# A masked copy moved from POOL to ACT in a fused sequence, attention and expert kernel

## The chip, the core and the metric

The kernel runs on one core of a Trainium2 chip. A core has a matrix engine (PE, whose weight loads are shown as PEld), a vector engine (DVE), an engine for activation functions (ACT), a general-purpose engine (POOL), and a queue engine (SP) that here only starts transfers. Each engine works through its own list of instructions in order; they wait for each other through counters (semaphores). PE writes its products into PSUM, eight banks of 512 float32 columns on 128 partitions. ACT and DVE read PSUM, POOL here reads and writes only SBUF. The metric is the device time of one execution in microseconds.

## The reference

The input is 128 sequences of 375 steps and 64 channels. Three blocks follow each other:

```
h = x
for i in 3 layers:                      # state-space layers
    dt, B, C = split(h @ W_dbc[i].T)    # 1 + 64 + 64 columns
    delta = softplus(dt * W_dt[i] + b_dt[i])
    hs = scan(exp(delta * A[i]) , delta * h * B)     # along time, 64 states
    h = sum_n(hs * C) + D[i] * h
    if i < 2: h = mean of neighbouring steps (375 -> 187 -> 93)
h = h + attention(layernorm(h))         # 8 heads, a polynomial of the scores, row-normalised
h = h + experts(layernorm(h))           # 6 experts of three layers, the 2 best are mixed
```

The router of the experts takes a softmax over six logits, the two largest probabilities, and a softmax over these two; with the difference of the two, its weights are 1/(1 + e) and e/(1 + e).

## The kernel before, in words

The 128 sequences are worked in 16 groups of eight. In a group there are four units of the state-space part: A and B are the first layer, four sequences each (744 columns of two banks); C is the second layer for all eight (744 columns), D the third (372 columns). Then follow "att" and "ffn" for the group. Layer 1 of group 5 may thus run while group 2 is in the experts. Only the first of the 64 states is scanned; the others are small enough that their part within one time step is a product with `m_quad`. A test at the end decides whether a general version has to run as well, which it doesn't for these inputs.

The order of the work is written out by hand, one list for each engine, in `ORDER` (line 222). An entry such as `B.three:4` is the step "three" of unit B in group 4; an entry of PE also names the PSUM bank that its product takes (`B.row:4/4`). Each step asks for what it needs with `need(g, ...)`; a wait is issued only if the counter has not been seen that far. Nothing overtakes within an engine.

The steps that matter here, for one unit:

- PE "row" (line 1235): the few projections of x that every channel needs (dt, and B and C of the first state) become rows, each of them three times, on partitions of one PSUM bank.
- ACT "row" (line 972) copies this bank to SBUF as float32, `rows`: 128 partitions, 186 columns (93 for D). DVE "most" takes a maximum of it for the test.
- POOL "three" (lines 879 to 885) splits the copies into three bfloat16 parts, so that a bfloat16 product can carry them: the masked high part, the difference, the masked middle part, and the last difference, which is `rows_three`. `row_mask` holds two columns of zeros and ones per partition, made by DVE in "prep.back".
- PE "dpre", "b" and "c" (line 1246) multiply `rows_three` by a matrix of zeros and ones and so spread each row over 64 channels.
- ACT "exp", "ln" and "decay" make delta and the decay; POOL "du" (line 889) is delta times x; DVE "vin", "scan" (line 1703), "base", "based" and "carry" (line 1716) make the output; POOL "y" (line 896) adds the two parts, and POOL "pooled" (line 904) adds neighbouring steps for the next layer.

SP loads x and swaps its halves (line 775). In attention, DVE makes normalised queries and keys (line 1762), POOL spreads the queries over the heads (`q_exp`, line 911), PE makes the scores (line 1348), ACT squares them (`pm`, line 1051), PE multiplies by the values (line 1361). In the experts, ACT makes the hidden layers (lines 1086 and 1093), DVE weights them (line 1818), PE makes the output (line 1456). DVE's "gate" (lines 1809 to 1813) turns the router's result into weights: `st` is a small SBUF tile, while `key` and `rsum` lie in the PSUM bank of the router's logits. POOL "split" (line 922) splits these weights as "three" splits the rows.

The wait that stands ahead of POOL's "three", and ACT's "row":

```
need(g_, f"act {u}.row")
need(0, "dve prep.back")
need(g_, f"pe {u}.dpre", f"pe {u}.b", f"pe {u}.c", back=1)
...
need(g, f"pe {u}.row")
need(g, f"pool {u}.three", f"dve {u}.most", back=1)
a.activation(rows[u][:], out_of(f"{u}.row", g)[:, 0, 0:WIDE[u] // 2], ACT.Copy).then_inc(me, 1)
```

Of the kernel before, what the change touches and what calls it, by code (L numbers as in the profile page):

```python
# [27 lines left out]
P = 128  # L28
# [8 lines left out]
def audio_tower(nc, x, A_log, Dp, W_dbc, W_dt, b_dt, Wqkv, bqkv, Wproj, bproj, temperature,  # L37
# [24 lines left out]
    with ctx:  # L62
# [88 lines left out]
        def per_unit(name, extra=0):  # L151
# [514 lines left out]
        def out_of(job, g):  # L666

            return ring[:, BANK[job, g]:BANK[job, g] + JOBS[job][0]]
# [813 lines left out]
        def _(dve):  # L1482
# [295 lines left out]
            def experts(g, u, s):  # L1778
                norm(g, u, s)

                def step(ins, name):

                    ins.then_inc(me, 1)
                    need(g, f"dve ffn.{name}")
# [76 lines left out]
```

## Time and profile before

| what | value |
|---|---|
| median of 3 timed runs | 685.24 us (682.52 to 686.23) |
| the profiled execution | 687.21 us |
| its span, first to last instruction | 685.4 us |
| mean granted clock of PE | 0.954 of full speed |
| PE / DVE / ACT / POOL busy | 583.1 / 560.9 / 517.7 / 470.6 us |
| HBM read, written | 13.25 MB, 3.05 MB |

The page and the trace come from one profiled execution. "Busy" is time in which an engine runs an instruction; waits on semaphores and starts of DMAs don't count. A matmul's end is modelled. The chain that ended last is followed back from the last instruction, at each step to what released it or to the instruction before it on its engine; "issue" on it is time for which the profile shows no wait. A wait for several counters is put down to the one that came last.

### The profile page before, as it was taken

Reading aid. Unit: us, or ns where it says so; the run is one execution under the profiler, and the core shown is the slowest. Engines: PE = TensorE matmul, PEld = TensorE weight load, DVE = VectorE, ACT = ScalarE, POOL = GpSimd, SP = SyncE. Lnnn points to the kernel's source line nnn. Section 1 sums busy time; section 2 is a strip of 40 time slices with the busy share of each in tenths; the row PEclk is TensorE's granted clock in tenths of the full one; section 3 lists DMA queues with packets and bytes.
Section 4 is the critical chain, followed back from the end, with each engine's and each line's share of the span. In section 5 each row is a group of like instructions: output and inputs, shape, how many; then the busy total and the mean of one; then the engine's idle time right before and its main releaser. Section 6 shows DMA issues by size and latency. Waiting matters only on the chain.

```text
span 685.4 us, 22980 instructions
## 1 busy us (share of the span) xinstructions
PE 583.1 (85%) x9595; PEld 306.5 (45%) x9595; DVE 560.9 (82%) x1097; ACT 517.7 (76%) x964; POOL 470.6 (69%) x564
## 2 busy tenths in 40 slices
PE   2857666889989898999999898998999988999983
PEld 1322233545445444554545444554545444545431
DVE  6799788889979798998998898999789888764551
ACT  1335548879969888998897887978888887897751
POOL 7769999889767778786886787786686775322000
PEclk9975879999999999999999999999999999999996
DMA  4422321221112202121211203121121000000001
GB/s 89 83 58 64 69 61 41 46 53 25 41 35 68 54 13 66 39 56 46 55 37 26 62 17 82 36 64 33 33 57 30 2 14 18 20 13 14 2 14 27
DMA packets 77576, 28.54 MB, mean 42 GB/s; under 512 B 69271, under 2 KB 77463, under 8 KB 77463
## 3 DMA queue, kind: packets, MB, share of 16 engines
q1 hardware_dynamic: 71290, 25.92, 16.5%
q10 hardware_dynamic: 6173, 1.05, 0.8%
q8 instruction: 78, 1.28, 0.8%
q14 instruction: 35, 0.29, 0.1%
HBM read 13.25 MB, written 3.05 MB: 24 GB/s over the span
## 4 chain that ended last, share of the span: by engine, by line
PE 45%; POOL 22%; ACT 12%; DVE 11%; issue 6%; DMA 2%; ACTq 1%; SPq 0%; POOLq 0%; DVEq 0%
PE ring L1260 6%; PE ring L1348 4%; PE ring L1361 4%; PE ring L1427 4%; PE ring L1436 4%; PE ring L1456 3%; ACT pm L1051 3%; PE ring L1246 3%; PE ring L1215 2%; PE ring L1235 2%; PE ring L1329 1%; ACT hid L1093 1%; PE ring L1270 1%; DVE ring L1707 1%; POOL q_exp L911 1%
## 5 line engine op out<-in xcount | busy, mean ns | idle before, releaser
L1051 ACT ACTIVATE pm<-ring,two_col 93x744 f32<-93x744 f32 x128 | 106.9, 872 | 13.1 <-PE ring L1348 12.0
L911 POOL TENSOR_TENSOR q_exp<-qk,mask_q 128x1488 f32<-128x1488 f32 x16 | 42.9, 2684 | 28.9 <-DVE qk L1762 28.9
L1348 PE MATMUL ring<-q_exp,qk 32*93 32x372 f32 x512 | 56.2, 507 | 7.4 <-POOL q_exp L911 0.9
L1086 ACT ACTIVATE hid<-ring,b_col 128x372 f32<-128x372 f32 x96 | 49.4, 567 | 7.7 <-PE ring L1436 6.3
L1818 DVE TENSOR_TENSOR hidw<-hid,ring 128x744 f32<-128x744 f32 x48 | 44.3, 922 | 12.2 <-PE ring L1417 8.9
L1361 PE MATMUL ring<-pm,v 97*32 97x93 f32 x2048 | 53.9, 247 | 0.1
L1361 PEld LDWEIGHTS ring<-pm,v 97*32 97x32 f32 x2048 | 42.9, 111 | 16.0 <-ACT pm L1051 4.8
L1093 ACT ACTIVATE hid<-ring,b_col 128x744 f32<-128x744 f32 x48 | 42.2, 878 | 7.4 <-PE ring L1427 5.4
L1427 PE MATMUL ring<-hid,w 64*64 64x372 f32 x384 | 40.9, 496 | 2.9 <-ACT hid L1086 2.0
L1436 PE MATMUL ring<-nrm_f,w 64*64 64x372 f32 x384 | 41.7, 505 | 0.7 <-ACT hid L1093 0.5
L896 POOL TENSOR_TENSOR base_C<-base_C,carry_C 128x744 f32<-128x744 f32 x16 | 28.5, 1780 | 18.0 <-DVE carry_C L1716 14.8
L896 POOL TENSOR_TENSOR base_A<-base_A,carry_A 128x744 f32<-128x744 f32 x16 | 28.3, 1770 | 11.4 <-DVE carry_A L1716 11.3
L1456 PE MATMUL ring<-hidw,w 128*64 128x372 f32 x192 | 34.3, 494 | 0.0
L889 POOL TENSOR_TENSOR du_A<-delta_A,x_A 128x744 f32<-128x744 f32 x16 | 28.7, 1797 | 7.7 <-ACT delta_A L989 7.7
L889 POOL TENSOR_TENSOR du_B<-delta_B,x_B 128x744 f32<-128x744 f32 x16 | 28.8, 1799 | 7.2 <-ACT delta_B L989 5.7
L889 POOL TENSOR_TENSOR du_C<-delta_C,x_C 128x744 f32<-128x744 f32 x16 | 28.8, 1797 | 6.9 <-ACT delta_C L989 6.9
L922 POOL CAST gate_part<-gate 93x144 bf16<-93x144 f32 x16 | 4.8, 302 | 38.8 <-DVE gate L1813 38.7
L896 POOL TENSOR_TENSOR base_B<-base_B,carry_B 128x744 f32<-128x744 f32 x16 | 28.4, 1775 | 3.0 <-DVE carry_B L1716 3.0
L1348 PEld LDWEIGHTS ring<-q_exp,qk 32*93 32x93 f32 x512 | 17.2, 154 | 26.1 <-issue 4.6
L1703 DVE TENSOR_TENSOR_SCAN carry_B<-dec_B,ring 128x744 f32<-128x744 f32 x16 | 27.2, 1700 | 0.3
L1703 DVE TENSOR_TENSOR_SCAN carry_A<-dec_A,ring 128x744 f32<-128x744 f32 x16 | 27.2, 1698 | 0.2
L1703 DVE TENSOR_TENSOR_SCAN carry_C<-dec_C,ring 128x744 f32<-128x744 f32 x16 | 27.1, 1693 | 0.1
(368 smaller groups left out, 1816.7 us busy)
## 6 DMA issues: line engine op xcount, KB each, us to landing
xin_A<-in_x_dram SPq DMA_DIRECT2D x62, 93.0 KB
xin_B<-in_x_dram SPq DMA_DIRECT2D x62, 93.0 KB
x_A<-x_A SPq DMA_DIRECT2D x32, 93.0 KB, 2.4
x_B<-x_B SPq DMA_DIRECT2D x32, 93.0 KB, 2.2
x_C<-x_C SPq DMA_DIRECT2D x32, 93.0 KB, 2.2
out_dram<-osb SPq DMA_DIRECT2D x15, 186.0 KB
x_D<-x_D SPq DMA_DIRECT2D x32, 46.5 KB, 1.9
w<-in_L_ffn_expert_w_dram SPq DMA_DIRECT2D x6, 48.0 KB
```

What stands on the lines that cost most here:

```text
L889: g.tensor_tensor(halves(du[u][:]), halves(delta[u][:]), xs[u][:, 0::2, :], ALU.mult).then_inc(me, 1)
L896: g.tensor_tensor(base[u][:], base[u][:], carry[u][:], ALU.add).then_inc(me, 1)
L911: g.tensor_tensor(q_exp[:], qk[:, 0, :].rearrange("p (q t) -> p q t", q=NPAIR)[:, :, None, :].broadcast_to(wide), mask_q[:, None, :, None] ...
L1051: a.activation(pm[q % 2][h][0:TOUT].rearrange("m a j n -> m a (j n)"), out_of(f"att.s{q}{h}", g)[0:TOUT, :, 0:COLS], ACT.Square, bias=two_ ...
L1086: ins = a.activation(hid1[:, h], out_of(f"ffn.h1_{k}", g)[:, h, 0:COLS], ACT.Relu, bias=b1_col[:, h, k:k + 1])
L1093: a.activation(hid2[:], out_of(f"ffn.h2_{k}", g)[:, :, 0:COLS], ACT.Relu, bias=b2_col[:, k:k + 1]).then_inc(me, 1)
L1348: ins = mm(o[h][0:TOUT, b, 0:COLS], qk[r:r + 32, 1, q * TOUT:(q + 1) * TOUT], q_exp[r:r + 32, q].rearrange("p j n -> p (j n)"), start=True ...
L1361: ins = mm(o[32 * j:32 * j + 32, 0, h * TOUT:h * TOUT + TOUT], rows[:, at:at + 32], pm[q % 2][h][:, b, j, :], start=(b == 0), stop=(b == 1 ...
L1427: ins = mm(o[to:to + E, h, 0:COLS], w2[r:r + E, k, h], hid1[r:r + E, h], start=True, stop=True, tile_position=(r, to))
L1436: ins = mm(o[E * i:E * i + E, h, 0:COLS], w1[E * h:E * h + E, 2 * k + i], hn[E * h:E * h + E, :], start=True, stop=True, tile_position=(E ...
L1456: ins = mm(o[E * h:E * h + E, 0, 0:COLS], w3[:, k], hidw[k][:, h], start=False, stop=True, skip_group_check=True, tile_position=(0, E * h))
L1703: v.tensor_tensor_scan(carry[u][:], dec[u][:], b_made(u, g), 0.0, ALU.mult, ALU.add).then_inc(me, 1)
```

## The change

ACT's "row" makes two copies of the PSUM bank: `rows` as before, and `rows_hi`, in bfloat16 and scaled by the first column of the mask. POOL's "three" loses its first product. Its second product becomes a tensor_tensor with the mask's column broadcast, where it was a tensor_scalar. The wait for the masks ("prep.back") moves from POOL to ACT. In the gate, the denominator goes to `rsum` in PSUM instead of a column of `st`. The lists of all five engines are written anew: the same entries in another order, and other banks in PE's list. No entry of PE, ACT, POOL or SP moves more than 9 places; on DVE a few of the test's and the preparation's steps move further (up to 38).

Of the lists, the first lines of three engines:

```
-            "dve": ("prep.back:0 prep.w0:0 prep.mean:0 prep.dec:0 prep.w1:0 prep.w2:0 A.quad:0 B.most:0 prep.qkvp:0 "
-                    "B.quad:0 A.most:0 B.base:0 B.vin:0 B.based:0 B.scan:0 A.base:0 A.vin:0 B.carry:0 A.based:0 A.scan:0 "
-                    "prep.late:0 A.carry:0 B.quad:1 B.vin:1 prep.cen:0 B.scan:1 B.base:1 A.quad:1 B.based:1 B.carry:1 "
...
+            "dve": ("prep.w0:0 prep.back:0 prep.w2:0 prep.mean:0 prep.w1:0 B.most:0 A.most:0 prep.qkvp:0 prep.dec:0 "
+                    "B.quad:0 A.quad:0 B.base:0 B.vin:0 B.based:0 A.base:0 A.based:0 A.vin:0 B.scan:0 prep.late:0 "
+                    "B.carry:0 A.scan:0 A.carry:0 B.vin:1 B.scan:1 B.quad:1 prep.cen:0 C.most:0 B.base:1 B.carry:1 "
...
-            "pool": ("prep.pads0:0 prep.masks0:0 prep.masks1:0 B.three:0 A.three:0 prep.pads1:0 B.du:0 A.du:0 prep.pads2:0 "
-                    "B.three:1 B.y:0 B.pooled:0 B.du:1 A.y:0 A.pooled:0 C.three:0 A.three:1 C.du:0 B.y:1 A.du:1 B.three:2 "
...
+            "pool": ("prep.masks0:0 prep.masks1:0 A.three:0 B.three:0 prep.pads2:0 prep.pads1:0 B.du:0 A.du:0 prep.pads0:0 "
+                    "B.three:1 B.du:1 B.y:0 A.y:0 B.pooled:0 A.pooled:0 C.three:0 A.three:1 C.du:0 B.y:1 A.du:1 B.three:2 "
...
-            "act": ("A.x:0 prep.l3:0 B.x:0 prep.exp:0 A.row:0 B.row:0 prep.l5:0 B.exp:0 B.ln:0 B.decay:0 A.exp:0 A.ln:0 "
-                    "prep.l2:0 B.x:1 B.row:1 A.decay:0 B.exp:1 B.ln:1 A.x:1 B.decay:1 A.row:1 C.row:0 C.exp:0 C.ln:0 "
...
+            "act": ("prep.l3:0 A.x:0 B.x:0 prep.exp:0 A.row:0 B.row:0 prep.l5:0 B.exp:0 A.exp:0 B.ln:0 A.ln:0 prep.l2:0 "
+                    "B.x:1 B.decay:0 B.row:1 A.decay:0 B.exp:1 B.ln:1 A.x:1 B.decay:1 C.row:0 A.row:1 C.exp:0 C.ln:0 "
...
```

The rest of the diff:

```
@@ -577,7 +576,7 @@
                  "dve ffn.top": ["sum", "rsum", "key0", "kmax0", "oh0", "rest", "m1", "eq1", "key1", "kmax1", "oh1", "diff"],
                  "dve ffn.gate": ["den", "r0", "w1", "w", "gate"],
                  "pool ffn.split": ["hi", "mid", "rest", "lo"]}
-        PARTS |= {f"pool {u}.three": ["hi", "left", "mid", "three"] for u in UNITS}
+        PARTS |= {f"pool {u}.three": ["left", "mid", "three"] for u in UNITS}
 
         SSM_STEPS = ["sp swap", "pe row", "act row", "dve most", "pool three", "pe dpre", "act exp", "act ln", "dve delta", "pool du", "act decay",
                      "pe z", "dve quad", "pe b", "dve vin", "dve scan", "pe s", "dve base", "dve based",
@@ -873,14 +872,11 @@
             def ssm(g_, u, s):
                 if s == "three":
                     need(g_, f"act {u}.row")
-                    need(0, "dve prep.back")
                     need(g_, f"pe {u}.dpre", f"pe {u}.b", f"pe {u}.c", back=1)
                     r, hi, left, three = (t_[u][:] for t_ in (rows, rows_hi, rows_left, rows_three))
-                    g.tensor_scalar(hi, r, row_mask[:, 0:1], None, ALU.mult).then_inc(me, 1)
-                    need(g_, f"pool {u}.hi")
                     g.tensor_tensor(left, r, hi, ALU.subtract).then_inc(me, 1)
                     need(g_, f"pool {u}.left")
-                    g.tensor_scalar(hi, left, row_mask[:, 1:2], None, ALU.mult).then_inc(me, 1)
+                    g.tensor_tensor(hi, left, row_mask[:, 1:2].broadcast_to([P, WIDE[u] // 2]), ALU.mult).then_inc(me, 1)
                     need(g_, f"pool {u}.mid")
                     g.tensor_tensor(three, left, hi, ALU.subtract).then_inc(me, 1)
                 if s == "du":
@@ -969,7 +965,10 @@
                 if s == "row":
                     need(g, f"pe {u}.row")
                     need(g, f"pool {u}.three", f"dve {u}.most", back=1)
-                    a.activation(rows[u][:], out_of(f"{u}.row", g)[:, 0, 0:WIDE[u] // 2], ACT.Copy).then_inc(me, 1)
+                    need(0, "dve prep.back")
+                    made = out_of(f"{u}.row", g)[:, 0, 0:WIDE[u] // 2]
+                    a.activation(rows[u][:], made, ACT.Copy)
+                    a.activation(rows_hi[u][:], made, ACT.Copy, scale=row_mask[:, 0:1]).then_inc(me, 1)
                 if s == "exp":
                     need(g, f"pe {u}.dpre")
                     need(0, f"dve prep.w{l}")
@@ -1806,8 +1805,8 @@
                 if s == "gate":
                     need(g, "act ffn.topexp")
                     need(g, "pool ffn.lo", back=1)
-                    step(ts(st[:, 0], st[:, 6], 1.0, None, ALU.add), "den")
-                    step(v.reciprocal(st[:, 1], st[:, 0]), "r0")
+                    step(ts(rsum, st[:, 6], 1.0, None, ALU.add), "den")
+                    step(v.reciprocal(st[:, 1], rsum), "r0")
                     step(tt(key, key, spread(st[:, 6]), ALU.mult), "w1")
                     step(tt(key, oh0[:], key, ALU.add), "w")
                     tt(gate[:], key, spread(st[:, 1]), ALU.mult).then_inc(me, 1)
```

## Rows read from the trace of the kernel before

**Rows 1.** The page's part 1: busy us, share of the span, instructions.

```profile
PE 583.1 (85%) x9595; PEld 306.5 (45%) x9595; DVE 560.9 (82%) x1097; ACT 517.7 (76%) x964; POOL 470.6 (69%) x564
```

**Rows 2.** The page's part 4: shares of the chain that ended last, by engine.

```profile
PE 45%; POOL 22%; ACT 12%; DVE 11%; issue 6%; DMA 2%; ACTq 1%; SPq 0%; POOLq 0%; DVEq 0%
```

**Rows 3.** Windows: length, busy us (instructions) of PE, PEld, DVE, ACT, POOL; granted clock, DMA.

```profile
40.00:120.00 80.00, 54.94 (x726) 26.15 (x727) 70.04 (x103) 44.20 (x71) 72.23 (x77) 0.77 0.25 58
120.00:340.00 220.00, 199.75 (x3579) 107.43 (x3579) 196.81 (x330) 188.62 (x354) 172.39 (x192) 0.99 0.20 45
340.00:560.00 220.00, 202.60 (x3512) 107.76 (x3515) 195.39 (x344) 186.37 (x352) 165.58 (x191) 0.99 0.17 39
560.00:640.00 80.00, 76.18 (x1341) 41.25 (x1333) 50.73 (x139) 68.59 (x139) 27.36 (x32) 1.00 0.07 16
```

**Rows 4.** The chain that ended last, in order of time: start us, us, what.

```profile
20.80 0.78 POOL rows_hi_B L879
...
48.77 0.34 ACT rows_C L972
...
49.19 0.77 POOL rows_hi_C L879
...
109.07 2.64 POOL q_exp L911
...
556.94 0.54 POOL rows_hi_D L879
```

**Rows 5.** Waits of PE's matmuls, 120 to 560 us: us in total, times, longest.

```profile
PE ring L1246 <- POOL rows_three_D L885: 5.5, 7, 2.2
PE ring L1246 <- POOL rows_three_C L885: 3.9, 6, 1.4
PE ring L1246 <- POOL rows_three_B L885: 2.1, 3, 0.8
```

**Rows 6.** Timeline of POOL: start us, us, what; one three of C, one of D.

```profile
49.19 0.76 POOL L879 TENSOR_SCALAR rows_hi_C<-rows_C,row_mask 128x186 bf16<-128x186 f32 x1 [1.07 <-ACT rows_C L972]
50.03 0.54 POOL L881 TENSOR_TENSOR rows_left_C<-rows_C,rows_hi_C 128x186 f32<-128x186 f32 x1
50.67 0.76 POOL L883 TENSOR_SCALAR rows_hi_C<-rows_left_C,row_mask 128x186 bf16<-128x186 f32 x1
51.51 0.54 POOL L885 TENSOR_TENSOR rows_three_C<-rows_left_C,rows_hi_C 128x186 bf16<-128x186 f32 x1
...
67.25 0.54 POOL L879 TENSOR_SCALAR rows_hi_D<-rows_D,row_mask 128x93 bf16<-128x93 f32 x1
67.88 0.36 POOL L881 TENSOR_TENSOR rows_left_D<-rows_D,rows_hi_D 128x93 f32<-128x93 f32 x1
68.33 0.53 POOL L883 TENSOR_SCALAR rows_hi_D<-rows_left_D,row_mask 128x93 bf16<-128x93 f32 x1
68.94 0.36 POOL L885 TENSOR_TENSOR rows_three_D<-rows_left_D,rows_hi_D 128x93 bf16<-128x93 f32 x1
```

**Rows 7.** Groups of ACT's instructions: busy us, mean ns, idle before and its releaser.

```profile
L972 ACT ACTIVATE rows_C<-ring 128x186 f32<-128x186 f32 x16 | 5.2, 324 | 8.4 <-PE ring L1235 8.0
...
L972 ACT ACTIVATE rows_D<-ring 128x93 f32<-128x93 f32 x16 | 3.9, 245 | 3.6 <-PE ring L1235 3.6
...
L1012 ACT ACTIVATE ln_rows_a<-ring,eps_col 128x93 f32<-128x93 f32 x16 | 5.4, 338 | 0.7 <-PE ring L1277 0.7
...
L1034 ACT ACTIVATE qk_norm<-qk_norm,ln_col 128x186 f32<-128x186 f32 x16 | 7.1, 446 | 0.1
```

**Rows 8.** Timeline at 571 us: POOL's q_exp and DVE's denominator.

```profile
571.50 2.68 POOL L911 TENSOR_TENSOR q_exp<-qk,mask_q 128x1488 f32<-128x1488 f32 x1 [0.77 <-DVE qk L1762]
...
571.76 2.45 DVE L1809 TENSOR_SCALAR st<-st 93x8 f32<-93x8 f32 x1 [0.34 <-ACT st L1080]
```

**Rows 9.** The denominator's line 1809: ns min/median/max, first and last start us.

```profile
L1809 DVE TENSOR_SCALAR st<-st x16: 156/167/2446, 164.0 to 661.7; 93x8 f32<-93x8 f32 x16
```

**Rows 10.** Groups of DVE's instructions: the gate's product step; busy us, mean ns.

```profile
L1811 DVE TENSOR_TENSOR ring<-ring,st 93x48 f32<-93x48 f32 x16 | 3.4, 212 | 0.6
```

More of the change, by code:

```diff
@@ L579, in audio_tower @@
                  "pool ffn.split": ["hi", "mid", "rest", "lo"]}
-        PARTS |= {f"pool {u}.three": ["hi", "left", "mid", "three"] for u in UNITS}
+        PARTS |= {f"pool {u}.three": ["left", "mid", "three"] for u in UNITS}
         SSM_STEPS = ["sp swap", "pe row", "act row", "dve most", "pool three", "pe dpre", "act exp", "act ln", "dve delta", "pool du", "act decay",
@@ L875, in ssm @@
                     need(g_, f"act {u}.row")
-                    need(0, "dve prep.back")
                     need(g_, f"pe {u}.dpre", f"pe {u}.b", f"pe {u}.c", back=1)
                     r, hi, left, three = (t_[u][:] for t_ in (rows, rows_hi, rows_left, rows_three))
-                    g.tensor_scalar(hi, r, row_mask[:, 0:1], None, ALU.mult).then_inc(me, 1)
-                    need(g_, f"pool {u}.hi")
                     g.tensor_tensor(left, r, hi, ALU.subtract).then_inc(me, 1)
                     need(g_, f"pool {u}.left")
-                    g.tensor_scalar(hi, left, row_mask[:, 1:2], None, ALU.mult).then_inc(me, 1)
+                    g.tensor_tensor(hi, left, row_mask[:, 1:2].broadcast_to([P, WIDE[u] // 2]), ALU.mult).then_inc(me, 1)
                     need(g_, f"pool {u}.mid")
@@ L971, in ssm @@
                     need(g, f"pool {u}.three", f"dve {u}.most", back=1)
-                    a.activation(rows[u][:], out_of(f"{u}.row", g)[:, 0, 0:WIDE[u] // 2], ACT.Copy).then_inc(me, 1)
+                    need(0, "dve prep.back")
+                    made = out_of(f"{u}.row", g)[:, 0, 0:WIDE[u] // 2]
+                    a.activation(rows[u][:], made, ACT.Copy)
+                    a.activation(rows_hi[u][:], made, ACT.Copy, scale=row_mask[:, 0:1]).then_inc(me, 1)
                 if s == "exp":
@@ L1808, in experts @@
                     need(g, "pool ffn.lo", back=1)
-                    step(ts(st[:, 0], st[:, 6], 1.0, None, ALU.add), "den")
-                    step(v.reciprocal(st[:, 1], st[:, 0]), "r0")
+                    step(ts(rsum, st[:, 6], 1.0, None, ALU.add), "den")
+                    step(v.reciprocal(st[:, 1], rsum), "r0")
                     step(tt(key, key, spread(st[:, 6]), ALU.mult), "w1")
```

623 rows, old and new, of the table ORDER are left out of this document.

## The prediction, made before the changed kernel was run

> **What bounds the kernel now.** I read the busy line of the page first [rows 1]: PE 583 us, DVE 561, ACT 518, POOL 471 of a 685.4 us span. No engine is full on average, and POOL looks least pressed. The shares of the chain that ended last say otherwise [rows 2]: POOL holds 22% of it and ACT 12%, DMA only 2%. The reader is to see that the "spare" engine is on the path.
>
> The stretches show where [rows 3]. From 40 to 120 us POOL is busy 72.2 of 80, DVE 70.0, PE only 54.9 (at a granted clock of 0.77). This stretch is POOL's. From 120 to 560 us PE is busy 199.75 + 202.60 = 402.4 of 440 (91%), DVE 392.2 (89%), ACT 375.0 (85%), POOL 338.0 (77%): PE first, with DVE and ACT close behind. From 560 to 640 PE has 76.2 of 80 and POOL hardly works.
>
> The chain of waits in order of time [rows 4] shows which POOL work it is. The first step of a "three" (line 879, the masked high part) stands on the chain 43 times of 64, first at 20.80 and last at 556.94 us; the pieces add up to 29.4 us. The pieces of the third step (line 883) add up to 28.3 us. Before 24 of the 43 stands ACT's copy of the rows, as at 48.77. So a row product on PE goes to ACT, POOL and back to PE, and the end of the kernel often hangs on that loop. PE's own waits agree [rows 5]: from 120 to 560 us its matmuls of line 1246 waited 5.5 + 3.9 + 2.1 = 11.5 us for rows_three, in 16 waits, out of 37.6 us of idle time.
>
> **The change part by part.** The sum is made against the profiled execution, 687.21 us (span 685.4 and 1.8 around it). The median of the three timed runs is 685.24, so I work out a difference and take it off the median.
>
> *POOL loses the masked high part and does the masked middle part as a tensor_tensor.* Step times from start to start are in the timeline [rows 6]. For a unit of 186 columns: the high part 50.03 - 49.19 = 0.84 us, the difference 0.64, the middle 0.84, the last 0.54. The first goes, and the middle should take a tensor_tensor's 0.64: 0.84 + 0.20 = 1.04 us saved. For D (93 columns): 0.63 + (0.61 - 0.45) = 0.79. With 48 wide and 16 D steps, 48 x 1.04 + 16 x 0.79 = 62.5 us of POOL. The new middle step has an operand that is broadcast, which none of these rows has. Lower bound: q_exp, with both operands broadcast, took 2.68 us for 1488 columns [rows 8], 1.80 ns each, so 0.34 for 186, and the saving would be about 73 us. Upper bound: it stays at the tensor_scalar's 0.76, and the saving is 48 x 0.84 + 16 x 0.63 = 50.4. I take the tensor_tensor rows, the nearest in size and type.
>
> Against this edit speaks a rule of the Trainium skill. The page "GPSIMD Engine Reference" (sections "Performance versus the Vector engine" and "Engine selection") has two-input elementwise work bound by a shared read port at about 2.5 cycles an element, and one-input work roughly at line rate. By it (an estimate from that page) the middle step would become some 0.2 us dearer, POOL would save about 37 us, and the forecast below would be 680. The trace disagrees: for the same 186 columns the two-input step took 0.54 and the one-input step 0.76 [rows 6].
>
> *ACT gets a second copy from PSUM, with a scale read per partition.* The copy without it took 324 ns at 186 columns and 245 at 93 [rows 7]. Line 1012, 93 columns from PSUM with one per-partition operand, took 338: 93 ns more. So 0.417 and 0.338 us, and 48 x 0.417 + 16 x 0.338 = 25.4 us on ACT. Bounds: no extra cost, 48 x 0.324 + 16 x 0.245 = 19.5; line 1034's 446 ns for the wide ones, 26.8. 48 of the 64 fall between 120 and 560 us: 36 x 0.417 + 12 x 0.338 = 19.1, which takes ACT there to 394 of 440 (90%). Queued behind the second copy are the Exp, Ln and square steps that PE and POOL wait for, and the bank of the row product comes free one copy later. ACT's first row step now also waits for the masks ("back"), which DVE makes after "w0" instead of before it; PE's first row product ends at about 20 us, later than that work can end, so I cost it at nothing. Without that cover it would cost 1 to 3 us at the start.
>
> *The loop.* From PE's row product to PE's "dpre" the wide way gets 1.04 - 0.42 = 0.62 us shorter and D's 0.79 - 0.34 = 0.45.
>
> *What it is worth, stretch by stretch.* From 40 to 120 us eleven threes start (nine wide, two of D; the one at 49.19 [rows 4] is the first): 9 x 1.04 + 2 x 0.79 = 10.9 us off the busiest engine. DVE's 70.0 us is what is late next, so at most 10 can come through; I take 5.5, half. From 20 to 40 us the first two threes lie on the chain back to back, each 0.6 shorter: 1. From 120 to 560 us the 16 waits of PE can give at most 9 x 0.62 + 7 x 0.45 = 8.7 us (nine of the wide units, seven of D); late next is DVE or the PE work itself, so I take a third, 3, and charge 1 for the copies that ACT puts ahead of work that PE awaits: 2 net.
>
> *The gates' denominator.* One of its 16 instances took 2.45 us where the median is 0.17 [rows 8, 9]: it began 0.26 us after POOL's q_exp and ended with it, at 574.2. The gate's product step, which writes PSUM, took 0.21 us on average over its 16 [rows 10], so was never held up so; I expect the same of a denominator written there. That is 2.3 us at most, and PE has only 3.8 us of idle time between 560 and 640 us. I take 1; bounds 0 and 2.3.
>
> *New orders.* PE's order moves 489 of 872 entries (by 8 places at most), ACT's 526 of 789 (9), DVE's 484 of 686, POOL's 132 of 277, SP's 76 of 115 (6). SP's loads and swaps pass each other by a few places; with DMA at 2% of the chain, and x loaded ahead of use, I cost that at nothing, and at one late swap (2 to 3 us) if the cover goes. DVE's "late" preparation moves ahead of the first carry of B, which holds POOL's first sum; it may dodge the POOL work that it ran beside. I set both against each other. The orders as a whole can cost or return, by PE's idle 37.6 us, perhaps a fifth of it either way, 7.5 us; I take nothing.
>
> Sum: -5.5 - 1 - 2 - 1 = -9.5, so 677.7 for the profiled execution and 676 against the median.
>
> **The rivals.** *The chain shortens and nothing takes its place.* The chain loses 29.4 + 43 x 0.08 (the gaps) and a quarter of 28.3, and gains 24 copies of 0.4: -30 us, 655. For it: the 43 pieces. Against: in two thirds of the span PE and DVE are at 90%.
>
> *Nothing comes of it.* POOL only waits longer, for DVE's carries and ACT's deltas, the start gains 2 to 3 and the rest stays: 683. For it: the span is PE's and DVE's from 120 us on, and neither does less.
>
> *ACT becomes the bound (the other side).* Place: 120 to 560 us, ACT's queue. Price: 19 us of copies ahead of the squares, Exps and relus that PE waits for in order. If 10 of the 19 reach the end and the start gives 3: 692; all of them: 701. It turns slower than before once more arrives than the start gives, about 3 us, and measurably so from about 6.5, a third of the copies. For it: ACT at 90% beside PE at 91%, each in a fixed order. Against: ACT had 65 us idle there.
>
> **How the numbers follow.** A difference under 0.5% (3.4 us) can't be told from none. The forecast's own range, 668 to 681.8, has 0.55; the shortened chain (under 668) 0.10; nothing 0.20; ACT 0.15. Faster 0.65, same 0.20, slower 0.15. The range runs from 664, part of the way into the shortened chain, to 690, most of the way into ACT's case; the orders' 7.5 us and the bounds of the middle step lie within it.
>
> **What would show it.** POOL busy about 410 us, ACT about 543; the middle step at 0.54 and 0.36; the second copy at 0.42 and 0.34; no denominator above 0.3 us. The first q_exp, at 109.07 us before [rows 4], should start near 102. PE's waits for rows_three from 120 to 560 us should fall from 11.5 to 7 or less. I am wrong if the first q_exp comes no earlier than 106, if the stretch from there to the last three is not shorter, or if PE's waits for ACT's squares and Exps grow by more than its waits for rows_three shrink.

## The result, and the profile after

The changed kernel takes 658.25 us, median of four runs (656.1 to 659.24), against 684.76 before: ratio 0.961, with an interval of 0.9577 to 0.9643. The forecast was 676 with a range from 664 to 690, so the direction was right and the size was not: 26.5 us instead of 9.5. The profiled execution took 659.24 us with a span of 657.5.

First the parts of the page that answer to [rows 1, 2] (busy us by engine; shares of the chain that ended last):

```profile
PE 582.7 (89%) x9595; PEld 308.3 (47%) x9595; DVE 553.2 (84%) x1097; ACT 531.6 (81%) x1028; POOL 410.6 (62%) x500
...
PE 54%; ACT 16%; DVE 10%; POOL 7%; issue 5%; DMA 1%; SPq 0%; POOLq 0%; ACTq 0%; DVEq 0%
```

POOL's busy time fell by 60 us to 410.6, as worked out; its share of the chain fell from 22% to 7%. PE has the same work as before and now stands on 54% of the chain. ACT's busy time rose by 13.9 us, not 25, in the main because the second copy overlaps the first (below).

The stretches, as in [rows 3] (length, busy us of PE, PEld, DVE, ACT, POOL; clock, DMA):

```profile
40.00:120.00 80.00, 61.63 (x864) 30.29 (x862) 70.41 (x93) 51.20 (x90) 67.38 (x72) 0.78 0.24 56
120.00:340.00 220.00, 209.69 (x3696) 114.50 (x3696) 203.59 (x359) 202.72 (x398) 156.07 (x178) 1.00 0.21 50
340.00:560.00 220.00, 211.64 (x3703) 112.75 (x3706) 200.30 (x354) 200.96 (x393) 143.91 (x163) 1.00 0.17 39
560.00:640.00 80.00, 73.84 (x1171) 37.73 (x1167) 45.91 (x147) 62.33 (x129) 16.61 (x25) 1.00 0.05 11
```

From 120 to 560 us PE is busy 421.3 of 440 us, where it was 402.4. These windows hold different work in the two kernels, since everything comes earlier in the second. For a fair comparison take the stretch from the start of the first q_exp to the start of the thirteenth, nearly the same work in both (the lists move a few steps over its edges). Before:

```profile
109.02:543.52 434.50, 396.38 (x6960) 212.32 (x6960) 386.25 (x666) 369.91 (x694) 336.50 (x380) 0.99 0.19 44
```

After:

```profile
104.29:519.67 415.38, 396.29 (x6979) 213.72 (x6977) 384.29 (x669) 382.60 (x744) 293.05 (x333) 1.00 0.20 46
```

PE is busy 396.4 and 396.3 us in them, but 434.5 us pass before and 415.4 after: PE's idle time went from 38.1 to 19.1 us. So the gain in span of 27.9 us lies thus: 4.7 up to the first q_exp (109.02 to 104.29), 19.1 in this stretch, 4.1 behind it.

PE's waits for rows_three in it before (us in total, times, longest), as in [rows 5]:

```profile
PE ring L1246 <- POOL rows_three_D L885: 4.7, 6, 2.2
PE ring L1246 <- POOL rows_three_C L885: 3.9, 6, 1.4
PE ring L1246 <- POOL rows_three_B L885: 3.2, 4, 1.0
```

And the longest of PE's waits in it after:

```profile
PE ring L1347 <- POOL q_exp L907: 1.3, 2, 0.9
PE ring L1259 <- DMA x_D<-x_D: 1.1, 2, 0.7
PE ring L1347 <- ACT pm L1050: 0.8, 1, 0.8
```

rows_three is not among PE's waits any more; what is left are pieces of a microsecond or so from all sides.

The single prices. POOL's three of C in the timeline, as [rows 6]; then the second copy on ACT (ns min/median/max), beside [rows 7]; then the denominator, beside [rows 9]:

```profile
47.56 0.54 POOL L877 TENSOR_TENSOR rows_left_C<-rows_C,rows_hi_C 128x186 f32<-128x186 f32 x1 [1.35 <-ACT rows_hi_C L971]
48.17 0.49 POOL L879 TENSOR_TENSOR rows_hi_C<-rows_left_C,row_mask 128x186 bf16<-128x186 f32 x1
48.75 0.54 POOL L881 TENSOR_TENSOR rows_three_C<-rows_left_C,rows_hi_C 128x186 bf16<-128x186 f32 x1
```

```profile
L971 ACT ACTIVATE rows_hi_C<-ring,row_mask x16: 407/411/438, 47.1 to 542.8; 128x186 bf16<-128x186 f32 x16
L971 ACT ACTIVATE rows_hi_D<-ring,row_mask x16: 331/336/353, 65.8 to 565.1; 128x93 bf16<-128x93 f32 x16
```

```profile
L1808 DVE TENSOR_SCALAR ring<-st x16: 152/156/167, 155.8 to 633.3; 93x8 f32<-93x8 f32 x16
```

The middle product takes 0.49 us (0.54 forecast, 0.76 before), the copy with a scale 0.411 and 0.336 (0.417 and 0.338 forecast), and no denominator is longer than 0.167. The chain now goes round the loop like this (compare [rows 4]):

```profile
46.85 0.33 ACT rows_C L970
...
47.17 0.31 ACT rows_hi_C L971
...
47.56 0.55 POOL rows_left_C L877
...
48.17 0.49 POOL rows_hi_C L879
...
48.75 0.55 POOL rows_three_C L881
...
104.33 2.64 POOL q_exp L907
```

From the rows copy to the end of the last product it takes 2.44 us (46.85 to 49.29, in the chain's and the timeline's times), where from 48.77 to 52.05 it was 3.28.

### The profile page after: what moved, and what is told of

It reads as the page before. It is cut to its first block, busy times and chain, and to the rows that moved or that the text cites. A ratio compares the mean times of both kernels' runs of the same rounds, so it can differ in the third digit from the quotient of the medians.

```text
span 657.5 us, 22993 instructions
## 1 busy us (share of the span) xinstructions
PE 582.7 (89%) x9595; PEld 308.3 (47%) x9595; DVE 553.2 (84%) x1097; ACT 531.6 (81%) x1028; POOL 410.6 (62%) x500
## 4 chain that ended last, share of the span: by engine, by line
PE 54%; ACT 16%; DVE 10%; POOL 7%; issue 5%; DMA 1%; SPq 0%; POOLq 0%; ACTq 0%; DVEq 0%
PE ring L1259 8%; PE ring L1347 5%; PE ring L1360 5%; PE ring L1455 4%; PE ring L1245 3%; PE ring L1426 3%; PE ring L1435 3%; ACT pm L1050 3%; PE ring L1234 2%; PE ring L1406 2%; DVE ring L1706 2%; PE ring L1328 2%; PE ring L1214 2%; PE ring L1302 2%; ACT hid L1085 2%
## 5 line engine op out<-in xcount | busy, mean ns | idle before, releaser
L1435 PE MATMUL ring<-nrm_f,w 64*64 64x372 f32 x384 | 40.3, 488 | 0.7 <-DVE gate L1812 0.3
L964 ACT ACTIVATE x_A<-ring 128x744 f32<-128x744 f32 x16 | 12.6, 787 | 19.6 <-issue 14.7
L1057 ACT ACTIVATE yT<-ring 128x186 f32<-128x186 f32 x64 | 20.9, 326 | 8.7 <-PE ring L1360 8.1
```

Source lines behind the costliest of these rows:

```text
L1435: ins = mm(o[E * i:E * i + E, h, 0:COLS], w1[E * h:E * h + E, 2 * k + i], hn[E * h:E * h + E, :], start=True, stop=True, tile_position=(E ...
```

## The experiments

Each ran three or more times beside the kernel before on the same chip. The changed kernel's ratio, 0.961, is the mark for those that start from it.

**The edits with the lists of before.**

```
         ORDER = {
-            (the five lists of the changed kernel)
+            (the five lists of before)
```

> All edits to instructions of the change, with the five lists and banks of before. Theory 1 (the edits: lighter POOL and a shorter loop shorten the chain under any order): 655 to 665 us, PE's idle time from 120 to 560 us near 19 us as in the changed kernel. Theory 2 (the lists: the same edits in the old order meet the old queueing): 676 to 686 us, PE still idle for 30 us or more there. Theory 3 (neither alone): 668 to 676 us.

668.08 us, ratio 0.9753 (0.9708 to 0.9799): 16.9 us gained, just inside the range of theory 3. PE's idle time from 120 to 560 us is 29.7 us, far from the 19 of theory 1. Its stretch from first to thirteenth q_exp, and the chain by engine:

```profile
104.31:526.86 422.55, 392.79 (x6952) 211.72 (x6949) 383.83 (x665) 379.29 (x741) 291.72 (x333) 1.00 0.20 45
```

```profile
PE 56%; ACT 19%; DVE 12%; issue 4%; DMA 4%; POOL 2%; SPq 1%; ACTq 1%; POOLq 0%; DVEq 0%
```

422.55 us for 392.8 of PE work: 12.0 us shorter than before. PE's waits for rows_three in this stretch were 11.8 us before and are down to one of 0.2 here. POOL holds only 2% of the chain. So with nothing but the edits, the middle stretch gives up nearly the whole of those waits.

That 12.0 and 11.8 are so close is chance. PE's idle time fell by 8.4 us (38.1 to 29.8), since other waits grew; the other 3.6 us are PE's busy time (396.4 to 392.8). Before, PE's granted clock fell twice in this stretch from full speed (2.4 GHz) to 0.50 (1.2 GHz), for 3.4 us each; with the edits it stays at 1.00. The first fall came behind PE's longest wait for rows_three, the second behind two shorter ones, of 0.77 us for rows_three and 0.87 for ACT:

```profile
198.72 0.28 PE L1246 MATMUL ring<-rows_three_D,row_back_dpre 64*64 64x93 bf16 x8 [2.22 <-POOL rows_three_D L885]
```

```profile
199.24:202.65 3.41, 3.41 (x52) 1.63 (x48) 1.93 (x2) 2.06 (x5) 2.16 (x5) 0.50 0.01 2
479.15:482.55 3.40, 3.40 (x38) 1.94 (x34) 2.65 (x2) 2.35 (x5) 3.40 (x3) 0.50 0.10 24
```

PE was busy all through these 6.8 us, at half speed; at full speed the work would take half, an estimate from these rows, so some 3.4 us of the gain came by the clock. No run separates it from the waits.

**The lists with the instructions of before.**

```
         ORDER = {
-            (the five lists of before)
+            (the five lists of the changed kernel)
```

> The instructions of before (four products on POOL, one copy on ACT, denominator in SBUF) with the five lists and banks of the changed kernel. Theory 1 (the edits): 680 to 692 us, no better than before. Theory 2 (the lists): 657 to 667 us. Theory 3 (the lists need the lighter POOL): 685 to 700 us, with PE's waits for rows_three longer than the 11.5 us of before.

686.18 us, ratio 1.0027 (1.0004 to 1.005). The lists alone gain nothing, they lose a trace. The stretch between the q_exps, and PE's waits for rows_three in it:

```profile
112.07:548.38 436.31, 400.64 (x6998) 214.20 (x6990) 387.80 (x671) 374.76 (x698) 338.14 (x381) 0.99 0.19 44
```

```profile
PE ring L1245 <- POOL rows_three_C L884: 7.0, 8, 1.6
PE ring L1245 <- POOL rows_three_B L884: 1.5, 3, 0.8
PE ring L1245 <- POOL rows_three_D L884: 1.1, 2, 0.8
```

436.3 us, with 9.6 us of those waits still there; theory 3 had expected more than the 11.5 of before, and they did not grow. The lists are worth +0.3% with the old instructions and -1.4% with the new ones (0.9753 to 0.961): the lists' part of the gain needs the edits, which is theory 3 for this part, though by another sign than the one expected. The banks in PE's list went with its order here; the two were not separated.

**The denominator alone, and all but the denominator.**

```
-                    step(ts(st[:, 0], st[:, 6], 1.0, None, ALU.add), "den")
-                    step(v.reciprocal(st[:, 1], st[:, 0]), "r0")
+                    step(ts(rsum, st[:, 6], 1.0, None, ALU.add), "den")
+                    step(v.reciprocal(st[:, 1], rsum), "r0")
```

> Before, with the gates' denominator alone moved into PSUM. If the hold-up by q_exp at 571 us is paid for at the end: 682 to 684 us, and no denominator longer than 0.3 us. If it only fills time in which DVE's results were not awaited: 684 to 686 us.

> The changed kernel with the denominator back in SBUF. If the denominator carries a part of the gain: 660 to 662 us, with one or more instances over 1 us. If it is worth nothing in the new order: 657 to 659 us.

In the kernel before: 683.98 us, ratio 0.9979 (0.9953 to 1.0006). Taken out of the changed kernel: 658.32 us, ratio 0.9607 (0.9557 to 0.9657), the same as with it. Worth nothing that can be measured, in either. But the first interval reaches from 0.4 us lost to 3.2 us gained, so the forecast 1 us is neither borne out nor ruled out, and the second run brought no such hold-up back: its longest denominator took 1.07 us. In the one profile of before, PE did pay for the 2.45 us of [rows 8], by waiting for the gate that they held up:

```profile
575.22 0.52 PE L1369 MATMUL ring<-yT,norm_rows 128*32 128x186 f32 x8 [1.80 <-DVE gate L1813]
```

With the denominator alone in PSUM, the profile shows no wait ahead of this step (572.98 us).

**The two edits of "three", each alone in the old lists.** First the middle product as a tensor_tensor alone, then the high part on ACT alone (POOL keeps the tensor_scalar for the middle):

```
-                    g.tensor_scalar(hi, left, row_mask[:, 1:2], None, ALU.mult).then_inc(me, 1)
+                    g.tensor_tensor(hi, left, row_mask[:, 1:2].broadcast_to([P, WIDE[u] // 2]), ALU.mult).then_inc(me, 1)
```

> Before, in the old order, with one edit: the masked middle product is a tensor_tensor with the mask's column broadcast (0.50 and 0.34 us in the changed kernel's trace, 0.76 and 0.53 before). The loop gets 0.26 us shorter, POOL is relieved of 64 such pieces, 15.4 us in all. If the chain shortens by its pieces (43 of 64 lie on it): 673 to 678 us. If the first product is what matters: 682 to 686.

```
-                    g.tensor_scalar(hi, r, row_mask[:, 0:1], None, ALU.mult).then_inc(me, 1)
-                    need(g_, f"pool {u}.hi")
...
+                    a.activation(rows[u][:], made, ACT.Copy)
+                    a.activation(rows_hi[u][:], made, ACT.Copy, scale=row_mask[:, 0:1]).then_inc(me, 1)
```

> Before, in the old order, with one edit: the masked high part is ACT's second copy, POOL keeps the middle product as a tensor_scalar; the denominator stays in SBUF. All edits together in this order gave -16.8 us. If the two edits add up by POOL time removed (0.84 against 0.27 us a step): 671 to 675 us. If by what the loop gets shorter (0.43 against 0.27 us): 673 to 678 us. If the loop alone counted and the second copy ate it: 680 or more.

The middle product alone: 674.66 us, ratio 0.9849 (0.9812 to 0.9886), 10.3 us for 15 us of POOL time. The high part alone: 671.38 us, ratio 0.979 (0.9754 to 0.9827), 14.4 us. Together they gave 16.9, not 24.7: either of them takes most of what the old lists have to give. PE's waits for rows_three between the q_exps show it, first with the middle product alone, then with the high part alone:

```profile
PE ring L1246 <- POOL rows_three_D L885: 2.5, 4, 1.5
PE ring L1246 <- POOL rows_three_B L885: 2.2, 5, 0.8
PE ring L1246 <- POOL rows_three_C L885: 1.6, 3, 0.9
```

```profile
PE ring L1246 <- POOL rows_three_D L882: 0.5, 2, 0.4
PE ring L1246 <- POOL rows_three_B L882: 0.2, 1, 0.2
```

11.8 us before, 6.3 with the one, 0.7 with the other, 0.2 with both. When these waits are gone, the old lists hold PE up elsewhere: its idle time there is 29.5 us with the high part alone and 29.8 with both.

**POOL's load against the loop's length.** An idle product of the size of the one removed, into a tile that nobody reads, is put back into the changed kernel: behind each three, then ahead of its first difference.

```
                     g.tensor_tensor(three, left, hi, ALU.subtract).then_inc(me, 1)
+                    g.tensor_scalar(junk[:, 0:WIDE[u] // 2], left, row_mask[:, 0:1], None, ALU.mult)
```

> The changed kernel with one idle POOL product more behind each three (a tensor_scalar into a tile that nobody reads, 0.76 us at 186 columns, 0.53 at 93; 46 to 54 us of POOL in all). The loop from PE to PE stays as it is in the changed kernel, POOL is about as busy as before. Theory L (POOL's load is what counted): 668 to 680 us. Theory P (the loop's length is what counted): 657 to 663 us.

```
+                    g.tensor_scalar(junk[:, 0:WIDE[u] // 2], r, row_mask[:, 0:1], None, ALU.mult)
                     g.tensor_tensor(left, r, hi, ALU.subtract).then_inc(me, 1)
```

> The same idle product ahead of the first difference of each three, so it also stands in the loop (0.84 us longer). Theory L: the same as with the product behind, within 3 us. Theory P: 670 to 682 us, 10 us or more above the run with it behind.

Behind: 667.55 us, ratio 0.9737 (0.9703 to 0.977). Ahead: 674.01 us, ratio 0.9841 (0.9807 to 0.9875). So 43 us more of POOL cost 1.27% (8.7 us) without a longer loop, and 7.1 us more when they also stand in it. Neither theory alone: over the whole time, load and length each carry about half of what these runs added. In the one profile of each it is uneven. With the load behind, the first q_exp comes 3.3 us later (107.58) and the stretch to the thirteenth is 8.3 longer (423.66); with it ahead, 5.9 later (110.20) and 9.8 longer (425.21). So in the middle stretch it is mostly the load. And with the load behind, PE waits there for rows_three only 0.2 us; it waits for other products of POOL, `h_in` (2.8), q_exp (2.3) and `x_C` (1.6). The page of the run with the load behind (POOL's share of the chain is back at 16%), and PE's waits for rows_three between the q_exps in the other:

```profile
PE 581.3 (87%) x9595; PEld 307.1 (46%) x9595; DVE 554.6 (83%) x1097; ACT 532.3 (80%) x1028; POOL 453.7 (68%) x564
...
PE 45%; POOL 16%; ACT 15%; DVE 10%; issue 5%; DMA 3%; SPq 3%; ACTq 2%; POOLq 0%; DVEq 0%
```

```profile
PE ring L1247 <- POOL rows_three_C L883: 2.4, 4, 0.8
PE ring L1247 <- POOL rows_three_B L883: 1.4, 4, 0.5
PE ring L1247 <- POOL rows_three_D L883: 0.7, 1, 0.7
```

**ACT: one more copy, one less.**

```
                     a.activation(rows_hi[u][:], made, ACT.Copy, scale=row_mask[:, 0:1]).then_inc(me, 1)
+                    a.activation(junk[u][:], (a constant tile), ACT.Copy, scale=row_mask[:, 0:1])
```

> The changed kernel with one idle ACT copy more behind each pair of copies (from and to SBUF, tiles that nobody waits for; about 0.4 us at 186 columns, 0.33 at 93; 20 to 25 us of ACT in all, of which some 14 as busy time where the copies overlap). The loop of the rows is not longer. If ACT at 92% between 120 and 560 us is a bound already: 668 to 678 us. If ACT's second copies hide in its idle time, as I costed them but for 1 us: 658 to 663 us.

```
-                    a.activation(rows[u][:], made, ACT.Copy)
-                    a.activation(rows_hi[u][:], made, ACT.Copy, scale=row_mask[:, 0:1]).then_inc(me, 1)
+                    if g % NG == 0:
+                        a.activation(rows_hi[u][:], made, ACT.Copy, scale=row_mask[:, 0:1])
+                    a.activation(rows[u][:], made, ACT.Copy).then_inc(me, 1)
```

> The changed kernel without ACT's second copy, but for the first group: it leaves out the high part of the rows, so that POOL subtracts a stale tile. 60 of 64 copies go, some 13 us of ACT's busy time, and the loop is 0.31 us shorter. If the copies are hidden, as I costed them (1 us): 656 to 658.5 us. If ACT's time counts at the price that one more copy had (8.4 us for 64): 648 to 653 us.

The second of these leaves out the high part of the rows behind the first group: POOL then subtracts a stale tile, so only its time means something, and its loop is a copy shorter too.

One more: 666.64 us, ratio 0.9739 (0.9694 to 0.9784), 8.8 us for 17 us of busy time. One less: 656.32 us, ratio 0.9607 (0.9582 to 0.9632), no gain clear of the noise. The copies that the change adds are hidden, as I had costed them; the next ones would not be. The page with one more copy shows ACT on 23% of the chain (16% in the changed kernel):

```profile
PE 582.4 (87%) x9595; PEld 306.6 (46%) x9595; DVE 553.5 (83%) x1097; ACT 548.6 (82%) x1092; POOL 411.0 (62%) x500
...
PE 44%; ACT 23%; DVE 12%; POOL 8%; issue 6%; DMA 2%; SPq 0%; POOLq 0%; ACTq 0%
```

**The middle product as a tensor_scalar in the new lists.** The edit of the middle product above, backwards.

> The changed kernel with the middle product as a tensor_scalar again (0.27 us more per three on POOL and in the loop). If each step's 0.27 us comes through as the chain had it before: 666 to 672 us. If the new lists leave slack for it: 658 to 663 us.

659.32 us, ratio 0.964 (0.9608 to 0.9673): not to be told from the changed kernel. What was worth 10.3 us alone in the old lists is worth some 2 in the new ones by the ratios (0.964 against 0.961), and some 5 at most with their intervals.

**Which lists.** PE's, ACT's or DVE's list can't be put back alone: the engines would wait for each other in a circle. POOL's and SP's can. Both, then each:

```
         ORDER = {
-            "pool": (new)   "sp": (new)
+            "pool": (of before)   "sp": (of before)
```

> The changed kernel with the lists of POOL and SP from before; those of PE (with its banks), ACT and DVE stay new. With all five lists of before the same edits took 668.1 us, with all new 658.3. If the order on POOL, the engine that was relieved, carries the lists' part: 664 to 670 us. If it lies with PE, ACT and DVE: 657 to 661 us.

> The changed kernel with POOL's list alone from before (SP's new). With both of before it took 692.6 us. If POOL's order carries it: 680 to 692 us, with PE or DVE waiting for POOL's sums and h_in. If SP's order does: 658 to 665 us.

> The changed kernel with SP's list alone from before. If SP's order is worth nothing, as I costed it (at most one late swap, 2 to 3 us): 657 to 661 us. If it carries the loss of both: 680 to 692 us, with PE waiting for x to land or swaps late in the chain.

Both: 692.6 us, ratio 1.0137 (1.0103 to 1.0171), slower than the kernel before, with all edits in it, and far outside both expected ranges. POOL's alone: 681.34 us, 0.9973 (0.9945 to 1.0001), 24.8 us lost. SP's alone: 673.09 us, 0.9821 (0.9772 to 0.9869), 14.4 us lost by an order that only starts transfers, between the two expected ranges. All five lists of before cost only 9.6 us. So these runs show what one old list costs among new ones that were made for another; they don't divide the lists' gain between the engines.

SP's timeline shows where it begins. In the changed kernel (start us, us):

```profile
46.23 1.10 SPq L774 DMA_DIRECT2D x_C<-x_C  x2
47.38 4.30 SPq L726 DMA_DIRECT2D xin_A<-in_x_dram  x4
53.59 4.10 SPq L726 DMA_DIRECT2D xin_B<-in_x_dram  x4
57.79 1.88 SPq L774 DMA_DIRECT2D x_B<-x_B  x2
```

With SP's list of before:

```profile
47.44 1.10 SPq L774 DMA_DIRECT2D x_C<-x_C  x2
55.12 4.36 SPq L726 DMA_DIRECT2D xin_B<-in_x_dram  x4
59.59 1.84 SPq L774 DMA_DIRECT2D x_B<-x_B  x2
61.48 4.53 SPq L726 DMA_DIRECT2D xin_A<-in_x_dram  x4
```

The load of A's third group (line 726, four transfers, 4.5 us of SP's time) stands ahead of the next load and swap of B in the one and behind them in the other, and there SP waits 6.6 us ahead of B's load for PE's transposes (line 1214). So A's load starts at 61.48 instead of 47.38 us. PE waits 4.6 us for it, and the stretch from 40 to 120 us has a granted clock of 0.64, not 0.78. SP's wait, PE's wait and the stretch:

```profile
SPq L726 <- PE ring L1214: 6.6, 1, 6.6
```

```profile
PE ring L1214 <- DMA xin_A<-in_x_dram: 4.6, 1, 4.6
```

```profile
40.00:120.00 80.00, 59.30 (x690) 28.43 (x694) 66.79 (x91) 43.27 (x75) 61.25 (x65) 0.64 0.25 59
```

The first q_exp starts at 111.62 us, 7.3 late. The rest is lost later: in this profile the stretch to the thirteenth is 9.1 us longer than in the changed kernel (424.4 us), and I have not followed it.

## Why the prediction was wrong, by its steps

- *The prices* were right: the new middle product, the copy with a scale, POOL's 410 us. Only ACT's busy time, forecast near 543, is 531.6, since its copies overlap.
- *From 40 to 120 us*: 5.5 + 1 forecast up to the first q_exp, 4.7 measured. DVE, called late next, is the busiest engine there now (70.4 of 80 us).
- *From 120 to 560 us*: this step failed. It said that PE's 16 waits "can give at most 9 x 0.62 + 7 x 0.45 = 8.7 us", took a third and charged 1 for ACT, "2 net". Between the same q_exps 19.1 us came, 12.0 of them with the edits in the old lists. The waits for rows_three fell from 11.8 to 0.2, where "7 or less" was expected.
  - I had let each wait shrink only by what the loop itself got shorter. But a three also starts late because POOL is still busy with the work ahead of it, and that queue got shorter too. Take the 36 threes of B, C and D in the stretch (PE never waited there for one of A). From the start of ACT's copy to the end of the last product the traces have 4.05 us on average before and 2.82 with the edits in the old lists. Of these 1.23 us, 0.49 is less time between ACT's last copy and POOL's first product; the copies and products themselves give 0.74, also more than forecast.
  - The rows of before held a sign of this that I misread. I put ACT's copy before 24 of the 43 first products on the chain. The chain holds 24 such copies, but only 17 of the 43 follow straight on one, and 25 on other work of POOL, 13 of these on another three.
  - The sum counted PE's waits alone. Some 3.4 of the 12.0 us came by PE's granted clock, as worked out above.
  - That POOL's load counts apart from the loop is also what the load put back behind the three shows: 8.7 us, though there PE waited for POOL's other products.
- *The orders*: "I take nothing". They gave 9.6 us more together with the edits, and nothing without. I had bounded them by a fifth of PE's idle time, 7.5 us. My counts of moved entries left out some steps of the experts: it is 589 of 1016 on PE and 603 of 885 on ACT, and ACT's "decay" of A in group 10 moves 11 places, not 9. SP's moves were costed "at nothing, and at one late swap (2 to 3 us)"; undone alone they cost 14.4 us, which prices one old list among four new ones.
- *ACT's charge* of 1 us was right within the noise, by the run with the second copies left out. One more copy per rows would cost 8.8 us; that run is still 25 us short of the rival in which ACT becomes the bound (692).
- *The denominator*: 1 forecast; the runs can't tell it from nothing. Behind the thirteenth q_exp 4.1 us came, 1.9 of them with the edits in the old lists (139.9 us instead of 141.8), by causes that I have not followed.
- *The rival that came closest* was the shortened chain, 655 us, to which I gave 0.10. What I held against it, that PE and DVE are at 90%, was no bound: PE is at 95% between the q_exps now (396.3 of 415.4). But it priced the edits alone, and with the old lists these gave 668: that its number is near is in part luck.

None of the signs by which I would have been wrong came: the first q_exp is earlier than 106 (104.29), the stretch behind it is shorter, and PE's waits there for ACT's squares stayed at 2.8 to 2.9 us, while those for its Exps did not grow. The direction and the place were right; the middle stretch and the orders were put far too low.

What stays open is which places in the lists, or which of PE's banks, carry the lists' part, since PE's, ACT's and DVE's lists could not be exchanged one by one.

## What to carry to other kernels

A wait of the bound engine for a loop through two others can go altogether when the engine in the middle is relieved, because its queue shortens as well as the loop; so bound the gain by the whole wait, and by the bound engine's idle time, not by the saving of one pass. Look also at the clock behind the waits: here some 3.4 us came back there. An order written for one set of step times can be worth little with another: here the new lists gave nothing with the old instructions and 9.6 us with the new ones. So after an edit that moves 60 us off an engine, try the lists anew, and measure them together with it. Try the price of an engine's time in the finished kernel by adding an idle instruction; here POOL's cost 0.2 us and ACT's 0.5 us for each us on average, though POOL was idle for 38% of the span and ACT for 19%.

## What the runs showed of the hardware

- On POOL a product of 128 x 186 float32 with a per-partition column, written as bfloat16, takes 0.76 us as a tensor_scalar and 0.50 as a tensor_tensor with the column broadcast. The Trainium skill ("GPSIMD Engine Reference", section "Engine selection") has the two-input form as the slow one; in these traces it is the fast one.
- ACT's two copies of one PSUM bank overlap: the second starts 0.22 us after a first of 0.33 (46.85 and 47.07 us in the timeline). 64 second copies, 25 us by their durations, added 13.9 us of busy time. The overlap within a pair, 0.11 us on average, makes 7 of the 11 us between; the rest is overlap with the instructions beside it, which I have not followed.
